# 128-column matmuls in place of 256-column ones in an edge-feature tensor product, and gather indices copied four chunks at a time

## The reference

```python
def tensor_product(x_e, sh, w, C):
    acc = sh[:, 0:1] * (x_e @ C[:, 0, :])
    for s in range(1, S):
        acc = acc + sh[:, s:s + 1] * (x_e @ C[:, s, :])
    return acc * w
...
x_dst = tfn_features[edge_dst]
wk = mlp2(edge_features, k_w1, k_b1, k_w2, k_b2)
wv = mlp2(edge_features, v_w1, v_b1, v_w2, v_b2)
k = tensor_product(x_dst, edge_sh, wk, Cqk)
v = tensor_product(x_dst, edge_sh, wv, Cv)
attn = einsum('ehd,ehd->eh', q[edge_src], k)
```

## Time and profile before

| | us |
|---|---|
| median of 3 runs | 5317.2 (5316.74 to 5322.68) |
| profiled execution, its own time | 5320.04 |
| span of that execution, first to last instruction | 5318.1 |
| PE busy | 4829.7 (91%) |
| PEld busy | 4517.3 (85%) |
| DVE busy | 4062.1 (76%) |
| POOL busy | 3756.6 (71%) |
| ACT busy | 3416.6 (64%) |

### The profile page before, as it was taken

The page is one execution under the profiler, slowest core; times in us unless marked ns, Lnnn a source line. Parts: engine busy times, 40 slices in busy tenths (PEclk is TensorE's granted clock), DMA queues, the critical chain, the costliest instruction groups (busy, mean ns, idle before and its releaser), DMA issues. The chain is left out here.

```text
span 5318.1 us, 116347 instructions
## 1 busy us (share of the span) xinstructions
PE 4829.7 (91%) x35582; PEld 4517.3 (85%) x35582; DVE 4062.1 (76%) x5044; ACT 3416.6 (64%) x6495; POOL 3756.6 (71%) x3788
## 2 busy tenths in 40 slices
PE   7999999999999999999999999999999999998256
PEld 6888899898899898899999889998988988988243
DVE  5878788787788887787888888787877878887335
ACT  2666666666666666666666666666666666666237
POOL 3777777777777777777777777777777777775370
PEclk9999999999999999999999999999999999999578
DMA  8898889889889998898988989898889989897320
GB/s 214 190 201 200 201 198 202 199 202 200 197 198 199 203 203 197 198 201 199 203 202 200 202 199 204 196 202 202 199 197 200 202 199 203 200 204 163 95 72 25
DMA packets 693459, 1006.46 MB, mean 189 GB/s; under 512 B 120054, under 2 KB 378168, under 8 KB 693160
## 3 DMA queue, kind: packets, MB, share of 16 engines
q1 hardware_dynamic: 574856, 753.93, 62.0%
q0 software_dynamic: 112960, 242.16, 21.3%
q10 hardware_dynamic: 5600, 9.83, 0.6%
HBM read 826.64 MB, written 178.93 MB: 189 GB/s over the span
## 5 line engine op out<-in xcount | busy, mean ns | idle before, releaser
L814 PE MATMUL psum<-chi,zhi 128*128 128x256 f32 x7840 | 2339.0, 305 | 1.7 <-DVE rv L720 1.5
L525 POOL DMA_INDIRECT gq<-qtab,idxs x1568 | 1838.2, 1172 | 478.0 <-issue 478.0
L817 PE MATMUL psum<-clo,zhi 128*128 128x256 f32 x7840 | 2148.7, 283 | 0.0
L520 POOL DMA_INDIRECT gx<-in_xg,idxs x1568 | 1549.5, 988 | 697.1 <-issue 374.1
L816 PE MATMUL psum<-chi,zlo 128*128 128x256 f32 x6272 | 1778.2, 284 | 0.0
L814 PEld LDWEIGHTS psum<-chi,zhi 128*128 128x128 f32 x7840 | 1498.0, 191 | 103.5 <-issue 103.5
L817 PEld LDWEIGHTS psum<-clo,zhi 128*128 128x128 f32 x7840 | 1496.2, 191 | 0.0
L674 DVE TENSOR_TENSOR z<-psum,shb 128x1536 f32<-128x1536 f32 (+1 forms) x784 | 1131.1, 1484 | 391.6 <-PE psum L786 381.5
L569 ACT ACTIVATE zhi<-z 128x1536 fp32r<-128x1536 f32 (+1 forms) x784 | 994.4, 1268 | 471.1 <-DVE z L674 464.4
L816 PEld LDWEIGHTS psum<-chi,zlo 128*128 128x128 f32 x6272 | 1200.0, 191 | 102.8 <-issue 102.8
L699 DVE TENSOR_TENSOR zlo<-z,zhi 128x1536 fp32r<-128x1536 f32 (+1 forms) x784 | 922.4, 1218 | 0.0
(11 more groups left out here) (210 smaller groups left out, 6555.5 us busy)
## 6 DMA issues: line engine op xcount, KB each, us to landing
shb<-in_shT SPq DMA_DIRECT2D x392, 640.0 KB
shb<-in_shT SPq DMA_DIRECT2D x392, 512.0 KB
rows<-ot SPq DMA_DIRECT2D x392, 416.0 KB
e<-in_eT SPq DMA_DIRECT2D x392, 128.0 KB
drow<-rankd SPq DMA_DIRECT2D x392, 128.0 KB
gx<-in_xg,idxs POOLq DMA_INDIRECT x1568
gq<-qtab,idxs POOLq DMA_INDIRECT x1568
qtab<-qs ACTq DMA_DIRECT2D x25, 256.0 KB, 5.7
```

The lines of the kernel that those rows point to most:

```text
L520: nc.gpsimd.indirect_dma_start(out=gx[:, s, k, :], out_offset=None, in_=xg[:, :], in_offset=bass.IndirectOffsetOnAxis(ap=idxs[:, s, k:k + ...
L525: nc.gpsimd.indirect_dma_start(out=gq[:, s, k, :], out_offset=None, in_=qtab[:, :], in_offset=bass.IndirectOffsetOnAxis(ap=idxs[:, s, TC + ...
L814: mm(tpb[:, k, :], zhi[:, s, j, e], chi[:, j, :], start=(j == 0), stop=False)
L817: last = mm(tpb[:, k, :], zhi[:, s, j, e], clo[:, j, :], start=False, stop=(j == ST - 1))
```

## The change

- The 256-column matmuls of the tensor product become two of 128 columns each: all of a chunk's key columns first (into one PSUM bank), then all value columns (into the other). Every slice of zhi and zlo is loaded as stationary operand once for the keys and once for the values. 112 matmuls in a chunk in place of 56.
- `tp_full` becomes `tpk_full` and `tpv_full`. PE waits for `kq_done` ahead of the keys and for `vv_done` ahead of the values. DVE does keys, scores, values in that order. What waited for `tp_full` to overwrite zhi and zlo waits for `tpv_full`.
- The copy of gather indices is made for four chunks at once (32 columns), one step ahead of its first use; POOL waits for it in one chunk of four.
- In `fin2` the sixteen semaphores and the shared one of the products become three, one for each engine, counted in the order of its program.

```diff
-            idxs = ms("idxs", [P, 4, 2 * TC], i32)
+            idxs = ms("idxs", [P, 2, GC * 2 * TC], i32)
...
-            tpb = psum[:, 2 * 512:4 * 512].rearrange("p (t w) -> p t w", w=KV)
+            tpb = psum[:, 2 * 512:4 * 512].rearrange("p (k t w) -> p k t w", k=2, w=O)
...
+                    def indices(g):
+                        nc.gpsimd.tensor_copy(idxs[:, g.r // GC % 2, :],
+                                              idx_all[:, bass.ds(g.value() * 2 * TC, GC * 2 * TC)]).then_inc(idx_made, 1)
...
-                        nc.gpsimd.tensor_copy(idxs[:, s, :], idx_all[:, bass.ds(c.value() * 2 * TC, 2 * TC)]).then_inc(idx_made, 1)
-                        pool.wait_ge(idx_made, c.value() + 1)
-                        pool.sem_inc(pool_passed, 1)
+                        if c.r % GC == GC - 1 and (c + 1).there():
+                            indices(c + 1)
+                        if c.r % GC == 0:
+                            pool.wait_ge(idx_made, c.turn(GC) + 1)
+                            pool.sem_inc(pool_passed, 1)
+                        at = c.r % GC * 2 * TC
+                        ids = idxs[:, c.r // GC % 2, at:at + 2 * TC]
...
-                            act.wait_ge(tp_full, c.value() - 1)
+                            act.wait_ge(tpv_full, c.value() - 1)
...
-                            dve.wait_ge(tp_full, n - 2)
+                            dve.wait_ge(tpv_full, n - 2)
...
-                    def keys_and_values(t):
+                    def keys(t):
                         s, n = t.slot(2), t.value() + 1
-                        dve.wait_ge(tp_full, n)
+                        dve.wait_ge(tpk_full, n)
                         dve.wait_ge(wkq_done, n)
                         if t.old(1):
                             dve.wait_ge(attn_done, n - 1)
-                        v.tensor_tensor(kq[:, :, :], tpb[:, :, 0:O], ww[:, s, :, 0:O], ALU.mult).then_inc(kq_done, 1)
+                        v.tensor_tensor(kq[:, :, :], tpb[:, 0, :, :], ww[:, s, :, 0:O], ALU.mult).then_inc(kq_done, 1)
+
+                    def values(t):
+                        s, n = t.slot(2), t.value() + 1
+                        dve.wait_ge(tpv_full, n)
                         if t.old(UN):
                             dve.wait_ge(sum_full, 2 * (n - UN))
-                        v.tensor_tensor(rv[:, t.slot(UN), :, 0:O], tpb[:, :, O:KV], ww[:, s, :, O:KV], ALU.mult).then_inc(vv_done, 1)
+                        v.tensor_tensor(rv[:, t.slot(UN), :, 0:O], tpb[:, 1, :, :], ww[:, s, :, O:KV], ALU.mult).then_inc(vv_done, 1)
...
                         if t.there():
-                            keys_and_values(t)
+                            keys(t)
                             scores(t)
+                            values(t)
...
-                        if t.old(1):
-                            pe.wait_ge(kq_done, n - 1)
-                            pe.wait_ge(vv_done, n - 1)
-                        for k in range(TC):
-                            e = slice(k * P, (k + 1) * P)
-                            for j in range(ST):
-                                mm(tpb[:, k, :], zhi[:, s, j, e], chi[:, j, :], start=(j == 0), stop=False)
-                                if j < ST - 1:
-                                    mm(tpb[:, k, :], zlo[:, s, j, e], chi[:, j, :], start=False, stop=False)
-                                last = mm(tpb[:, k, :], zhi[:, s, j, e], clo[:, j, :], start=False, stop=(j == ST - 1))
-                        last.then_inc(tp_full, 1)
+                        for kind, o in enumerate((slice(0, O), slice(O, KV))):
+                            if t.old(1):
+                                pe.wait_ge((kq_done, vv_done)[kind], n - 1)
+                            for k in range(TC):
+                                e, to = slice(k * P, (k + 1) * P), tpb[:, kind, k, :]
+                                for j in range(ST):
+                                    mm(to, zhi[:, s, j, e], chi[:, j, o], start=(j == 0), stop=False)
+                                    if j < ST - 1:
+                                        mm(to, zlo[:, s, j, e], chi[:, j, o], start=False, stop=False)
+                                    last = mm(to, zhi[:, s, j, e], clo[:, j, o], start=False, stop=(j == ST - 1))
+                            last.then_inc((tpk_full, tpv_full)[kind], 1)
...
+            MADE = {"pe": ("mean", "var", "z0", "z1", "z2", "mean2", "var2"),
+                    "act": ("r", "sq", "lg", "rs", "h0", "h1", "sq2", "lg2", "rs2"),
+                    "dve": ("y", "dd", "x1", "s0", "y2", "dd2", "o")}
```

More of the change, by code:

```diff
@@ L414, in gnn_kernel @@
             shb_zero = sem("shb_zero")
-            idx_made, x_full, h_full, w_full, tp_full = (
-                sem("idx_made"), sem("x_full"), sem("h_full"), sem("w_full"), sem("tp_full"))
+            idx_made, x_full, h_full, w_full, tpk_full, tpv_full = (
+                sem("idx_made"), sem("x_full"), sem("h_full"), sem("w_full"), sem("tpk_full"), sem("tpv_full"))
             z_done, zhi_done, zlo_done = sem("z_done"), sem("zhi_done"), sem("zlo_done")
@@ L521, in gathers @@
                                 out=gx[:, s, k, :], out_offset=None, in_=xg[:, :],
-                                in_offset=bass.IndirectOffsetOnAxis(ap=idxs[:, s, k:k + 1], axis=0),
+                                in_offset=bass.IndirectOffsetOnAxis(ap=ids[:, k:k + 1], axis=0),
                             ).then_inc(x_in[s], 16)
@@ L526, in gathers @@
                                 out=gq[:, s, k, :], out_offset=None, in_=qtab[:, :],
-                                in_offset=bass.IndirectOffsetOnAxis(ap=idxs[:, s, TC + k:TC + k + 1], axis=0),
+                                in_offset=bass.IndirectOffsetOnAxis(ap=ids[:, TC + k:TC + k + 1], axis=0),
                             ).then_inc(q_in[s], 16)
+                    indices(Chunk(0, 0))
                     gathers(Chunk(0, 0))
@@ L1074, in gnn_kernel @@
             st_d, st_a, st_pe = sem("stats_dve"), sem("stats_act"), sem("stats_pe")
[L1075 to L1078, removed]
+            MADE = {"pe": ("mean", "var", "z0", "z1", "z2", "mean2", "var2"),
+                    "act": ("r", "sq", "lg", "rs", "h0", "h1", "sq2", "lg2", "rs2"),
+                    "dve": ("y", "dd", "x1", "s0", "y2", "dd2", "o")}
+            made_by = {e: sem(f"blocks_made_by_{e}") for e in MADE}
             def wait_made(engine, name, i, j):
[L1082 to L1085, removed]
+                for e, names in MADE.items():
+                    if name in names:
+                        engine.wait_ge(made_by[e], (i * len(names) + names.index(name)) * GN + (j + 1))
             with ExitStack() as fin1:
@@ L1264, in turn @@
                             for j in range(GN):
-                                sp.wait_ge(SS["o"], i * GN + (j + 1))
+                                wait_made(sp, "o", i, j)
                                 sp.dma_start(out[:, ncols(i, j)], W("sq", j)).then_inc(y_s[j], 16)
@@ L1282, in product @@
                                 wait_made(pe, after, i, j)
-                                t.matmul(bank_of(j), lhsT[:, :], W(src, j), start=True, stop=True).then_inc(prod_made, 1)
+                                t.matmul(bank_of(j), lhsT[:, :], W(src, j), start=True, stop=True).then_inc(made_by["pe"], 1)
                         def turn(i):
@@ L1315, in each_block @@
                                 wait_made(act, after, i, j)
-                                fn(j).then_inc(SS[name], 1)
+                                fn(j).then_inc(made_by["act"], 1)
                         act.wait_ge(st_d, 6)
@@ L1322, in turn @@
                                 if past(i):
-                                    act.wait_ge(SS["o"], i * GN)
-                                f(W("r", j), xp[:, ncols(i, j)], ACT.Identity, bias=st[:, 9:10]).then_inc(SS["r"], 1)
+                                    wait_made(act, "o", i + (-1), GN - 1)
+                                f(W("r", j), xp[:, ncols(i, j)], ACT.Identity, bias=st[:, 9:10]).then_inc(made_by["act"], 1)
                             for j in range(GN):
@@ L1327, in turn @@
                                     act.wait_ge(y_s[j], i * 16)
-                                act.wait_ge(SS["dd"], i * GN + (j + 1))
-                                f(W("sq", j), W("dd", j), ACT.Square).then_inc(SS["sq"], 1)
+                                wait_made(act, "dd", i, j)
+                                f(W("sq", j), W("dd", j), ACT.Square).then_inc(made_by["act"], 1)
                             each_block("lg", "var", lambda j: f(W("lg", j), bank_of(j), ACT.Ln, bias=epsc[:, 0:1]), i)
@@ L1361, in each_block @@
                                 wait_made(dve, after, i, j)
-                                fn(j).then_inc(SS[name], 1)
+                                fn(j).then_inc(made_by["dve"], 1)
                         def turn(i):
```

## The result

| | median us | runs |
|---|---|---|
| before | 5319.9 (5316.7 to 5323.7) | 4 |
| changed | 7606.4 (7600.2 to 7621.1) | 4 |

The ratio is 1.430, 95% interval 1.428 to 1.433: 43% slower, 7,620 was forecast. The profiled execution of the changed kernel has a span of 7599.1 us.

The account below looks back on a forecast made before the run. POOL's gather issue bounds the kernel before; doubled weight loads then make PE set 11.74 + 6.61 = 18.35 us a chunk (18.1 without lower-clock stretches). Times 392, plus 480.8 and 1.9: 7,676 or 7,578, taken as 7,620; range 7,120 to 12,000.

Parts of the forecast that it names:

- POOL, 71% busy, has no slack: Chunk stage before: POOL's gather issue sets the pace, 11.98 of 12.35 us a chunk accounted for; PE 0.6 us below.
- The weight load sets the pitch: Tensor products: loading 128 weights takes 0.11 to 0.118 us whatever the columns; 112 products cost 13.2 us, 6.6 more.
- The reading at half clock: Two products of two columns each end 0.22 us apart at half clock; at full clock that would be 0.11.
- 256 columns at 1.2 GHz and nothing more: Products before, at the lower clock: their 0.213 us pitch was read as the time of the columns only.
- The lower clock and the stop: Chunk stage: lower-clock stretches lose PE about 0.25 us a chunk before, perhaps none after; no stop was forecast.
- 18.1 if it loses them because it no longer waits: PE's us a chunk after the change if its lower-clock stretches vanish with its waits; 18.35 if they stay.
- The sum: Whole kernel: 392 chunks of 18.1 to 18.35 us, plus 480.8 around the stage and 1.9; 7,620 taken.
- The other edits: Index copy frees 0.84 us a chunk of POOL, worth nothing if PE needs 18; split semaphore and fin2 semaphores gain zero.
- Four cycles a column: Rival: float32r at 128 columns runs as slowly as plain float32, pitch 0.216 us, 11,890 us in all; 18%.
- A shorter load: Rival: the weight load takes 0.096 us or less, giving 6,610 us, span 5,300 to 7,100; 7%.
- Columns alone: Rival: only columns count, pitch 0.059 us, products cost 6.6 us a chunk as now, 5,089 us, 4.3% faster; 8%.
- The clock: Rival: PE's clock stays at 1.2 GHz, product pitch 0.213 us, 13,700 us, or 11,750 if only products run so; 7%.

Follow-up runs that it names:

- kernel 1: The kernel before with only the gather indices copied for four chunks at once, products left at 256 columns: 5026.0 us, ratio 0.949.
- kernel 4: The changed kernel with each of its 112 products cut to 64 moving columns, weight loads unchanged: 11,023 us, ratio 2.077.
- kernel 2: The changed kernel with the old index copy of every chunk and the old semaphores of the last stage: 7596.1 us, ratio 1.432.
- kernel 6: The changed kernel with key and value products of the same stationary operand placed next to each other: 7615.0 us, ratio 1.434.
- kernel 9: The changed kernel without its value products, 56 products of 128 columns in a chunk: 4941.1 us, ratio 0.931.
- kernel 8: The kernel before with its 56 products of 256 columns made twice over, 112 in a chunk: 7737.9 us, ratio 1.457.
- kernel 5: The changed kernel with each of its 112 stationary operands cut to 64 columns, 128 moving columns kept: 5365.5 us, ratio 1.010.

## Why the prediction was right, point by point

**What bounds the kernel.** Right. "POOL, 71% busy, has no slack" is shown by kernel 1: the copy for four chunks takes 0.94 us a chunk from POOL (1.12 less 0.18; 0.84 was forecast) and gave 0.76 us a chunk to the kernel. PE, next in line, took over at 11.55 us (11.49 forecast).

**The weight load sets the pitch.** Right, and shown from both sides: with 128 weights, 64, 128 and 256 moving columns run at 0.112, 0.112 and 0.118 us; with 64 weights, 128 columns run at 0.060. The size was off. The prediction took 0.118 for the load; it is 0.112, and 256 columns come to 0.007 us more. That they do so because their own 0.107 is so near is likely and not shown. In the sum, 112 products are 12.5 us a chunk and not 13.2: 0.7 us too much, 275 us in all. The reading at half clock, 0.22 us between two products of two columns, was the better one: halved, it is 0.11. Another reading was too narrow: the 0.213 at the lower clock was taken as "256 columns at 1.2 GHz and nothing more", but kernel 4 has 0.213 with 64 columns, so it is the load's time as well.

**The lower clock and the stop.** The prediction allowed 0 to 0.25 us a chunk for stretches at the lower clock and nothing for a stop. Measured are 164 us at half speed in 3000, which is 82 us lost or 0.50 us a chunk, and 53.6 us of stops, 0.32 a chunk. The step that failed is "18.1 if it loses them because it no longer waits": PE did lose its waits for gathered x, and got a stop at each turn of the loop instead. Each of the 20 spells at the lower clock from 1000 to 4000 us begins within 1 us of the end of such a stop. The stop at 3174.7 us and what follows it:

```profile
3174.70:3177.30 2.60, 0.01 (x1) 0.02 (x1) 0.00 (x0) 2.18 (x6) 0.00 (x0) 1.00 0.20 61
3177.30:3181.00 3.70, 3.70 (x13) 2.67 (x14) 2.44 (x2) 0.83 (x2) 0.00 (x0) 0.54 0.38 126
```

Stop and fetches of instructions come and go together over all eleven kernels, and in the changed kernel one of the eleven fetches of each turn starts within 0.5 us of the stop's start. That the fetches cause the stop was not tried by itself.

**The sum.** 4.9 for the rest + 12.5 + 0.5 + 0.3 = 18.2 us against 18.15 measured and 18.1 to 18.35 forecast. The pitch was 0.7 us too dear and the stop and clock 0.6 to 0.8 too cheap. That the forecast lies within 14 us of the median is luck: two errors of like size had opposite signs, and each alone would have missed by 3 to 4%.

**The other edits.** POOL's copy: nothing beside the products (kernel 2), as forecast, 5% without them. The semaphores of the last stage: nothing, 121.4 against 121.3 us. Keys first: DVE does what it was said to do, here beside value products that PE runs until 3027.6 us:

```profile
3023.64 0.69 DVE L728 TENSOR_TENSOR kq<-psum,ww 128x512 f32<-128x512 f32 x1
3024.36 0.69 DVE L742 TENSOR_REDUCE attn<-kq 128x32 f32<-128x512 f32 x1
3027.89 0.69 DVE L735 TENSOR_TENSOR rv<-psum,ww 128x512 f32<-128x512 f32 x1 [2.84 <-PE psum L833]
```

and it gains nothing (kernel 6), because PE never waited for it.

**The rivals.** Four cycles a column: out, the pitch is 0.112 with 128 and with 64. A shorter load: out, 0.112 is not "0.096 or less". Columns alone: out, kernel 9 has half the columns of kernel 1 and is only 1.7% faster. The clock: from 1000 to 4000 us it falls in the changed kernel only after a stop, but it is slower to come back after a stop, and it does fall at 64. 7% was little for a behaviour of which the trace of before had no row.

**The rule of the Trainium skill.** "TensorE: Matmul & The Clock Gate" in the Trainium skill, section "LDWEIGHTS (loading the stationary operand)", gives a load as its number of columns divided by 1.2 GHz, an estimate of 0.107 us for 128. The trace agrees at the full clock to 5% (0.112). It does not at the lower one, 0.213 for 128 weights beside 64 columns (kernel 4). So the load goes with the granted clock: 0.213 us are 256 cycles of 1.2 GHz and 0.112 are 268 of 2.4 GHz, about two cycles a weight column for these float32r operands. The Trainium skill, same page, section "Back-to-back issue gap", gives 81 ns for pairs at 128 columns, which were not seen here: the pitch is 112 ns.

**The version to keep** is kernel 1, 5026 us: the index copy for four chunks and the products as they were. It is 5.1% under the kernel before and 34% under the changed one.

## What to carry to other kernels

Splitting a matmul along its moving columns doubles its weight loads; before doing it, find out whether the pitch is that of the columns or of the load. Here the pitch was a little above the columns' time at the full clock (0.118 against 0.107) and equal to it at the lower one (0.213). The load was about as long as the columns, and half the columns were hardly cheaper, 0.112. Whether such a pitch is a sign of this in other kernels, one case does not show. And ask of an engine that issues DMAs how much of its time its sequencer takes between them: GpSimd at 71% busy set the pace, and a small edit there gave the 5% that a rewrite of the products could not.

## What the runs showed that was not expected

- The clock can fall to 1.2 GHz while TensorE is busy without a gap: in every chunk with products of 64 columns (kernel 4), never from 1000 to 4000 us with 56 of 128 (kernel 9). From 1000 to 4000 us it stayed up after a stop with 256 columns or came back after 3.4 us (kernel 8, 21 stops), and with 128 columns it stayed down for 27.3 us after four of 20 stops (changed kernel).
- With 84 or more products in each chunk of the eight in the loop, instructions are fetched all through the stage (441 fetches with 84 and 538 with 112, 22 with 56), and TensorE stops at the turns: for 2.7 us, 5.1 where the body runs through faster (kernel 5), 1.2 where it runs through slower (kernel 4). Among the kernels with 112 products, the faster TensorE gets through a body, the longer it stands, as it would if the fetch of instructions had a pace of its own. That is a guess, which no run tried.
- Loading weights again that are in place costs the full 0.112 us (kernel 6).
- One copy of 32 index columns on GpSimd takes 0.72 us (kernel 1; 0.22 in kernel 9), one of eight 0.31; per chunk, that is 0.18 against 0.31, and the larger part of the gain is the wait behind it, 0.81 us a chunk.
